# A fused audio tower on one core: the router's sigmoid by tanh, fewer small steps, and two states scaled by B on TensorE through diagonal matrices

## What is computed

```python
# 1. attention inside each segment, q = k = v
probs = softmax(einsum('bsqd,bskd->bsqk', x, x) / sqrt(256)); h = einsum('bsqk,bskd->bsqd', probs, x)
# 2. a selective scan on layernorm(h), 512 channels, 16 states n
x_in, z = split(xn @ W_in.T); x_conv = silu(conv4(x_in) + b_conv)
dt = softplus(x_conv @ W_dt.T + b_dt); B = x_conv @ W_B.T; C = x_conv @ W_C.T
state[n] = exp(dt * A[n]) * state[n] + dt * B[n] * x_conv;   y += C[n] * state[n]
h = h + (y * silu(z)) @ W_out.T
# 3. a mixture of 64 experts on layernorm(h)
scores = sigmoid(logits); sfc = scores + gate_bias     # 8 groups of 8 experts
# a group's score is the sum of its two best sfc; 4 groups are kept, then the 8 best experts of them
# weights: the kept scores over their sum, times 2.5; each expert runs silu(g) * u @ w_down
```

## Time and profile before

| | before |
|---|---|
| median of three runs | 3476.5 us (3473.83 to 3476.91) |
| the profiled execution | 3474.01 us, of which span 3472.2 us |
| PE busy | 2993.6 us, 86% |
| DVE busy | 2874.4 us, 83% |
| ACT busy | 2853.9 us, 82% |
| POOL busy | 2104.8 us, 61% |
| PE clock granted, mean | 0.955 |

### The profile page before, as it was taken

The page is one execution under the profiler, slowest core; times in us unless marked ns, Lnnn a source line. Parts: engine busy times, 40 slices in busy tenths (PEclk is TensorE's granted clock), DMA queues, the critical chain, the costliest instruction groups (busy, mean ns, idle before and its releaser), DMA issues. The chain is left out here.

```text
span 3472.2 us, 62460 instructions
## 1 busy us (share of the span) xinstructions
PE 2993.6 (86%) x19009; PEld 2407.9 (69%) x19009; DVE 2874.4 (83%) x4756; ACT 2853.9 (82%) x5580; POOL 2104.8 (61%) x780
## 2 busy tenths in 40 slices
PE   6899999999999999999999999999999997576664
PEld 4777777777777777777777777777777776455543
DVE  3888999999989999999999999999999998444432
ACT  5999999999999999999999999999999995211110
POOL 0666665666656565656565666666666665177776
PEclk8999999999999999999999999999999998578887
DMA  2111222111212121112221211111211110267774
GB/s 92 51 51 60 62 62 63 50 57 62 62 63 62 54 62 48 54 61 62 63 62 63 62 59 57 63 62 63 62 63 62 58 53 27 89 142 150 149 150 81
DMA packets 187542, 241.44 MB, mean 70 GB/s; under 512 B 45152, under 2 KB 165440, under 8 KB 187200
## 3 DMA queue, kind: packets, MB, share of 16 engines
q1 hardware_dynamic: 162624, 199.44, 18.5%
q0 software_dynamic: 24576, 37.77, 6.5%
HBM read 176.07 MB, written 61.08 MB: 68 GB/s over the span
## 5 line engine op out<-in xcount | busy, mean ns | idle before, releaser
L356 POOL TENSOR_TENSOR hid<-hid,c_all 128x1536 f32<-128x1536 f32 x512 | 1770.2, 3457 | 1160.9 <-DVEq L610 1159.4
L615 DVE TENSOR_TENSOR_SCAN hid<-decay,hid,psB 128x1024 f32<-128x1024 f32 x512 | 1201.6, 2347 | 101.8 <-PE psB L926 60.4
L386 ACT ACTIVATE decay<-dt,a_neg 128x383 f32<-128x383 f32 x2048 | 1086.7, 607 | 0.0
L374 ACT ACTIVATE dbu_t<-dtu_t,b_t 128x512 f32<-128x512 f32 x1536 | 994.6, 715 | 41.6 <-PE psB L926 38.1
L926 PE MATMUL psB<-ident,dbu_t 128*128 128x128 f32 x6144 | 856.9, 276 | 109.8 <-DVE hid L615 103.8
L926 PEld LDWEIGHTS psB<-ident,dbu_t 128*128 128x128 f32 x6144 | 701.5, 141 | 234.6 <-DVE hid L615 133.3
L938 PE MATMUL psY<-ident,hid 128*128 128x128 f32 x6144 | 765.3, 275 | 4.0 <-DVE yz_t L627 3.6
L938 PEld LDWEIGHTS psY<-ident,hid 128*128 128x128 f32 x6144 | 695.3, 142 | 6.9 <-issue 3.8
L615 DVE TENSOR_TENSOR_SCAN hid<-decay,psB 128x512 f32<-128x512 f32 x512 | 623.8, 1218 | 72.4 <-PE psB L926 29.7
L1013 PE MATMUL psM<-u,w_dt 128*128 128x384 f32 x1024 | 355.0, 490 | 21.2 <-ACT turned L396 16.8
L1013 PEld LDWEIGHTS psM<-u,w_dt 128*128 128x128 f32 x1024 | 184.4, 190 | 131.4 <-ACT turned L396 23.7
(11 more groups left out here) (149 smaller groups left out, 3348.3 us busy)
## 6 DMA issues: line engine op xcount, KB each, us to landing
c_all<-bc_rows_dram SPq DMA_DIRECT2D x128, 768.0 KB, 4.8
out_dram<-h SPq DMA_DIRECT2D x64, 384.0 KB, 5.6
h<-out_dram SPq DMA_DIRECT2D x32, 384.0 KB, 4.0
x_weights_dram<-normed SPq DMA_DIRECT2D x32, 384.0 KB, 3.3
xs<-in_x_dram SPq DMA_DIRECT2D x32, 256.0 KB
e_wg<-in_gate_dram SPq DMA_DIRECT2D x64, 128.0 KB
e_wu<-in_up_dram SPq DMA_DIRECT2D x64, 128.0 KB
e_wd<-in_down_dram SPq DMA_DIRECT2D x64, 128.0 KB
```

The source lines that it names most:

```text
L356: nc.gpsimd.tensor_tensor(hid[k % 4][:, :, :], hid[k % 4][:, :, :], c_all[:, k, :].unsqueeze(1).to_broadcast([P, CH, L]), ALU.mult).then_i ...
L374: last = nc.scalar.activation(dbu_t[k % 2][:, t, :], dtu_t[q][:, t, :], ACT.Copy, scale=b_t[q][:, t, k:k + 1])
L386: last = nc.scalar.activation(decay[k % 4][:, c, 1:L], dt[q][:, c, 1:L], ACT.Exp, scale=a_neg[:, c, k:k + 1])
L615: nc.vector.tensor_tensor_scan(h[:, lo:hi], flat(decay[k % 4])[:, lo:hi], flat(psB)[:, lo:hi], h[:, lo - 1:lo] if j else 0.0, ALU.mult, AL ...
```

## The change

1. **B by diagonal matrices.** For the states in `DIAG`, which are two of the 16 (4 and 10), ACT does no `scaled_dbu`. DVE writes `diag` (L734 of the changed kernel): for each such state and segment, the identity times B of the row, in a new step `spread_b`, once a sequence. PE forms the block of `psB` as a full matmul of `dtu_t` with the diagonal matrix instead of a transpose of `dbu_t`.
2. **Sigmoid.** ACT computes tanh(logit / 2) while the silu table is loaded, and DVE does one multiply-add; the add of one and the reciprocal go. For that, LG moves from slot 15 of sequence b - 2 to slot 4 of b - 3.
3. **Fewer small steps.** Newton's step for the norm takes three DVE instructions, not four. The row maximum is negated by the reduction itself, since 1/sqrt(D) now sits in the copies of QT0 and QT1. `score_groups` joins maxima that have the same operation.
4. **Softplus.** The four `Abs` on PSUM pieces become two on 128 x 768 in SBUF.
5. **Order.** O1 moves from slot 0 to slot 15 (its add to slot 0), the norm and routing on DVE one slot earlier, QT1 and its copy, `softplus(n, 0)`, `finish_dt(n, r, 0)` and the copies of xin, yz and dtu by up to one slot.

```diff
+DIAG = (4, 10,)
@@ scaled_dbu
                 after(act, s_bt, PB * (s - 1))
+                if k in DIAG:
+                    return
@@ DVE
+            def spread_b(n, r):
+                dve.wait_ge(s_out[slot("BT")], number("BT", n))
+                for i, k in enumerate(DIAG):
+                    last = nc.vector.tensor_tensor(diag[:, i, :, :], ident[:, :].unsqueeze(1).to_broadcast([P, NSEG, P]),
+                                                   b_t[r][:, :, k:k + 1].to_broadcast([P, NSEG, P]), ALU.mult)
+                last.then_inc(s_dg, 1)
@@ turn_dbu
-                    last = nc.tensor.transpose(flat(psB)[:, i * P:(i + 1) * P],
-                                               dbu_t[k % 2][:, t, c * P:(c + 1) * P], ident[:, :])
+                    if k in DIAG:
+                        last = nc.tensor.matmul(flat(psB)[:, i * P:(i + 1) * P], dtu_t[q][:, t, c * P:(c + 1) * P],
+                                                diag[:, DIAG.index(k), t, :], start=True, stop=True)
+                    else:
+                        last = nc.tensor.transpose(flat(psB)[:, i * P:(i + 1) * P],
+                                                   dbu_t[k % 2][:, t, c * P:(c + 1) * P], ident[:, :])
@@ ACT
-                nc.scalar.activation(soft[:, c, :], src, ACT.Abs, bias=b_dt[:, c:c + 1]).then_inc(s_out[slot(name)], 1)
+                nc.scalar.activation(soft[:, a:z, :], xin[:, a:z, TAPS - 1:], ACT.Abs).then_inc(s_de[half], 1)
-                    "p (s e) -> p s e", s=NSEG), ACT.Exp, scale=-1.0).then_inc(s_out[slot("LG")], 1)
+                    "p (s e) -> p s e", s=NSEG), ACT.Tanh, scale=0.5).then_inc(s_out[slot("LG")], 1)
@@ score_experts
-                nc.vector.tensor_scalar(flat(denom), flat(denom), 1.0, None, ALU.add).then_inc(s_rt, 1)
-                nc.vector.reciprocal(flat(score), flat(denom)).then_inc(s_rt, 1)
+                nc.vector.tensor_scalar(flat(score), flat(denom), 0.5, 0.5, ALU.mult, ALU.add).then_inc(s_rt, 1)
@@ newton
-                nc.vector.tensor_scalar(t[:, 2, :], t[:, 1, :], -0.5, 1.5, ALU.mult, ALU.add).then_inc(s_nw[j], 1)
@@ row_max
-                nc.vector.tensor_scalar(nmax[:, :], rmax[:, :], -(D ** -0.5), None, ALU.mult).then_inc(s_nm, 1)
```

More of the change, by code:

```diff
@@ L48, in after, with scaled_before @@
     eng.wait_ge(sem, count)
[L51 to L54, removed]
+DIAG = (4, 10,)
+SCALED = NS - len(DIAG)
+def scaled_before(k):
+    return k - sum(d < k for d in DIAG)
+SLOTTED = (("XN0", "X0", "X2", "Z0", "Z2", "D0", "D1", "D2", "D3", "X2T0", "AT0", "BT", "DU1", "DU2", "O1"),
+           ("XN1", "X1", "X3", "Z1", "LG", "QT0", "QT1", "S", "PT", "CB", "X2T1", "AT1", "YT0", "DU0", "YT1",
+            "YT2", "O0"))
 LAG = {**dict.fromkeys(("QT0", "QT1", "S", "PT", "AT0", "AT1",), 2),
@@ L109, in sequence_phase @@
         c_all = sb("c_all", [P, NS, L])
+        diag = sb("diag", [P, max(len(DIAG), 1), NSEG, P])
         decay = [sb(f"decay{j}", [P, CH, L]) for j in range(4)]
@@ L139, in sequence_phase @@
         rs0 = [sb(f"rs0{j}", [P, NSEG]) for j in range(2)]
-        nw = [sb(f"nw{j}", [P, 3, NSEG]) for j in range(2)]
+        nw = [sb(f"nw{j}", [P, 2, NSEG]) for j in range(2)]
         rstd = [sb(f"rstd{j}", [P, NSEG]) for j in range(2)]
@@ L395, in copy_turned @@
                 to = turned2 if name in ("X2T0", "X2T1") else turned
-                nc.scalar.activation(to[:, kd, :], psM[slot(name)][:, 0:L], ACT.Copy).then_inc(s_out[slot(name)], 1)
+                by = D ** -0.25 if name in ("QT0", "QT1") else 1.0
+                nc.scalar.activation(to[:, kd, :], psM[slot(name)][:, 0:L], ACT.Copy,
+                                     scale=by).then_inc(s_out[slot(name)], 1)
             def copy_xin(b, c):
@@ L421, in biased_dt @@
                 src = psM[slot(name)][:, 0:L]
-                nc.scalar.activation(xin[:, c, TAPS - 1:], src, ACT.Identity, bias=b_dt[:, c:c + 1])
-                nc.scalar.activation(soft[:, c, :], src, ACT.Abs, bias=b_dt[:, c:c + 1]).then_inc(s_out[slot(name)], 1)
+                nc.scalar.activation(xin[:, c, TAPS - 1:], src, ACT.Identity,
+                                     bias=b_dt[:, c:c + 1]).then_inc(s_out[slot(name)], 1)
             def softplus(n, half):
@@ L535, in body @@
                         if front:
+                            copy_xin(n, 1)
+                        if late:
+                            first_rstd(o, 1)
+                        if front:
                             copy_xin(n, 2)
@@ L550, in body @@
                             biased_dt(n, 1)
+                        if early:
+                            copy_turned("QT1", a, 1)
+                        if front:
+                            softplus(n, 0)
                     if k == 7:
@@ L553, in body @@
                             biased_dt(n, 2)
-                            softplus(n, 0)
-                        if late:
-                            copy_turned("X2T0", o, 0)
+                        if early:
+                            probs(a)
                     if k == 8:
@@ L751, in score_groups @@
-            def score_groups(m):
-                hi, lo = halves[:, 0, :, :], halves[:, 1, :, :]
-                hi2, mn, mx, lo2 = (quarters[:, j, :, :] for j in range(4))
+                routed_to(m, 2)
+                grp = biased[:, :, :].rearrange("p t (g h k) -> p (t g) h k", g=G, h=2)
+                nc.vector.tensor_tensor(halves[:, 0, :, :], grp[:, :, 0, :], grp[:, :, 1, :], ALU.max)
+                nc.vector.tensor_tensor(halves[:, 1, :, :], grp[:, :, 0, :], grp[:, :, 1, :], ALU.min).then_inc(s_rt, 1)
@@ L838, in body @@
                         nc.vector.engine_nop().then_inc(s_go, 1)
+                    if k == 0:
+                        if late:
+                            add_block(o, 1)
                     if k == 1:
                         if late:
[L841 removed]
                             second_stats(o)
@@ L1118, in body @@
                     if k == 8:
-                        if late:
-                            turn_normed2(o, 0)
                         if front:
@@ L1125, in body @@
                     if k == 9:
+                        if late:
+                            turn_normed2(o, 0)
                         if front:
```

192 lines of the change are left out of this document (93 added, 99 removed).

## The result

The changed kernel takes 3452.95 us in the median of four runs (3450.26 to 3454.04), the kernel before beside it 3476.7. The ratio is 0.9932, with a 95% interval of 0.9915 to 0.9949. That is 24 us faster. The profiled execution took 3450.26 us, of which the span is 3448.2. Against the profiled execution before (3474.01) it is 24 us too; forecast from there were 49.

A forecast was written before the change was run, and what follows sets the result against it. ACT was taken as the bound, DVE and PE close behind. Per sequence -0.3 and -1.3 make -1.6, over 31 sequences -50 us; with +1 at the end, 3474.0 becomes 3425 us, 8-in-10 range 3400 to 3481.

The forecast's parts named there:

- The step that failed: In the scan loop, ACT, idle 1.1 and 1.4 us in the two stretches, was taken as the bound.
- The dense stretch: Scan loop from PE's work at state 2 to state 10: 49.48 us to become 49.2, -0.3, with PE the bound.
- 48.9: PE's work in us between states 2 and 10 after the change: 45.7 before plus 3.2.
- 3.8 us of waits: PE's waits between states 2 and 10 before the change, the 49.48 us less 45.7 of work, expected to shrink to about 0.3.
- The light stretch: Scan loop from state 10 to the next state 2: DVE binds, 40.2 us to become 38.9, -1.3.
- 0.3 of waits: Allowance in us between state 10 and the next state 2, on top of DVE's 38.6, giving 38.9.
- The loop's turn stays: At the scan loop's turn no change in time was forecast; all gain was put in the 31 sequences.
- The end: After the last silu: two table loads on the last norm's chain +2.6, shorter last routing -1.6, sum +1 us.
- D: Rival: ACT still waits for the turning of state k - 2, halving the gain to 3450; counted with the forecast, together 0.71.
- A: Rival: PE's waits between states 2 and 10 stay, making the kernel slower, 3509 with 3.0 us left; chance 0.12.
- B: Rival: exchange without gain, PE waits of 1.5 to 2.2 us or DVE's ring remaining, within 7 us of 3474; chance 0.13.
- C: Rival: ACT alone bounds the scan loop, so the period falls by its full 3.8 us, to 3357; chance 0.04.

The follow-up runs named there:

- d_4: The changed kernel with only state 4 by a diagonal matrix instead of states 4 and 10: 3442.37 us, ratio 0.9907.
- d_10: The changed kernel with only state 10 by a diagonal matrix instead of states 4 and 10: 3471.33 us, ratio 0.9988.
- no state: The changed kernel without diagonal matrices and without spread_b, ACT scaling all 16 states again: 3456.5 us, ratio 0.9944.
- before_lg1: The kernel before with half of the router's product left out, 0.7 us less for PE, for timing alone: 3464.61 us, ratio 0.9976.
- before_norecip: The kernel before with the sigmoid's reciprocal replaced by a multiplication, 1.0 us less for DVE, for timing alone: 3463.92 us, ratio 0.9975.
- act_all: The changed kernel with ACT also scaling states 4 and 10, into a tile nobody reads, PE still using the diagonal matrices: 3485.13 us, ratio 1.0028.
- old_diag: The kernel before with only the diagonal matrices of states 4 and 10 added, in the old order: 3485.63 us, ratio 1.0036.
- After_lg1: The changed kernel with half of the router's product left out, 0.7 us less for PE, for timing alone: 3436.89 us, ratio 0.9897.
- d_3: The changed kernel with only state 3 by a diagonal matrix, instead of states 4 and 10: 3473.41 us, ratio 0.9997.
- Before_small: The kernel before with only the shorter Newton step and the negated row maximum, in the old order: 3472.63 us, ratio 0.9995.

## Why the prediction was off

**The costs.** Diagonal blocks 0.112 us apart, the multiplications on `diag` 0.543 us, `dbu_t` 14 times a sequence (1344 in all), two `Abs` at 0.85: all as forecast, and no table load at the tanh inside the loop. A state on `diag` keeps PE busy 195.8 / 64 = 3.06 us, against 752.8 / 448 = 1.68 for one of the other 14, a difference of 1.38 as forecast. The busy time of the engines moved less than the sums. ACT's fell by 3.1 us a sequence and not by 3.8: d_4 and d_10 have it 1.6 and 1.5 below no state, where 1.84 a state was put. PE's rose by 2.2 and not by 2.8, DVE's fell by 0.6 and not by 1.05. Where the rest went wasn't followed up.

**The step that failed** is the first: "ACT idles 1.1 and 1.4 us, less than either of the others, so ACT is the bound". From it came that both stretches shorten once ACT is relieved. In the kernel before, before_lg1 and before_norecip left ACT's work alone, and the ordinary period fell all the same by 0.26 and 0.32 us, which it could not if ACT's work alone set it. In the changed kernel, act_all measured the relief alone at 0.96 us for 3.1 removed, and the price on the other side at 1.13. (The relief alone was not measured in the kernel before; old_diag has relief and price together, +0.57.) The least idle engine was one of three that hand work round a ring: DVE scans a piece, PE may turn the next, ACT may write the one after. Removing work on one of them shows where another was waiting for it at that moment, and by the rows of no state these places are the X copies and the silu of Z. Ahead of them lies state 4's `dbu_t`, not state 10's.

**The dense stretch.** That PE becomes its bound was right, and PE busy over 98% too (49.58 of 49.90). The size of its work was not: "48.9" should be 49.6. The rows could have told: the earlier trace rows has PE busy 46.9 to 47.1 us in this stretch where the sum by the pace of each kind gave 45.7, and with the 3.2 forecast on top that is over 50 (2.6 came). What the prediction called 3.8 us of waits, to be won back, was 2.5 of idle time. So the stretch rose from 49.48 to 49.9 instead of falling by 0.3. After_lg1, with 0.7 us of PE's work less, has an ordinary period 0.52 shorter, which agrees with the bound. ACT idles 3.5 us there, less than the 4 forecast.

**The light stretch.** "That is -1.3" was wrong. My 40.2 for it before was too long, as its edges were not those of the 49.48: the ordinary period of 89.2 less the dense 49.48 leaves 39.7. After, 89.13 - 49.9 = 39.2. So -0.5 came, not -1.3. What was left as "0.3 of waits" is the wait for state 10's longer pieces alone, at 6.5 / 12 = 0.54 a sequence. The prediction's last sentence named this danger, DVE waiting at state 10; it had trusted DVE's work in those slots to hide it. For state 4 it does (no such wait is among the rows of d_4), for state 10 it does not.

**The loop's turn.** "The loop's turn stays" was wrong by 1.5 us a turn, some 19 in all, and this carries most of the gain. That the total came to half of the forecast is therefore luck: it is another gain than the one worked out. O1's new place explains the slot wait that is gone. It does not explain the turn: with O1 put back, the excess over an ordinary sequence is 1.16, not 2.35. State 10 has a part in it: the excess is 0.89 with it (changed kernel, d_10, act_all) and 1.22 to 1.31 without (no state, d_4, d_3), and old_diag has 1.67 in the old order. The rest, from 2.35 to 1.22, comes with the new order or the smaller parts, not with a shorter branch. Before_small, with two of the small steps, has 2.74 and so doesn't show it. Which part it is wasn't separated and stays open.

**The end.** Forecast were +1, measured are -3.9: from the last silu to the end of the scan 134.4 us pass in both kernels, and from there to the count phase 51.5 instead of 55.4. The phases behind it, which the change doesn't touch, were another 1.9 us shorter in the profile. Of the two table loads put on the chain, the one ahead of `lnv` is not on it. Timeline of ACT in the changed kernel:

```profile
2926.64 1.28 ACT L490 ACT_TABLE_LOAD   x1
2936.12 0.30 ACT L490 ACTIVATE lnv<-mv,epsc 128x3 f32<-128x3 f32 x1 [8.20 <-DVE mv L657]
2936.44 1.28 ACT L492 ACT_TABLE_LOAD   x1
2937.74 0.20 ACT L492 ACTIVATE rs<-lnv 128x3 f32<-128x3 f32 x1
```

The first load passes during a wait of 8.2 us for DVE. The second costs 1.30, from its start to that of the next. The Trainium skill, page "ScalarE: Activation LUTs", section "What ACT_TABLE_LOAD costs", counts 2.66 us with a drain; this row disagrees with that again. How the 3.9 us are made up wasn't tried.

**The rivals.** D hit the size (half, 3450) by luck, and not the cause: what ACT's relief gave was taken by the price on PE and DVE, and the gain that came is at the turns. A had the right sign for the dense stretch, which got longer, but with waits that did not stay. B, an exchange without gain, is what the ordinary sequences did. C is refuted by act_all: 3.1 us of ACT's work are worth 0.96.

## What to carry to other kernels

Where three engines hand work round a ring, the least idle of them is not yet the bound: look up, slot by slot, who waits for it, and relieve it only directly ahead of those waits. Before a trade between engines is spread over several places, try each place alone; here one state alone was worth -14 us and another +15. Read a loop's periods with a turn, right behind one, and away from one apart, and look which results share a PSUM slot before moving one.

## What was not expected of the hardware

- PE's branch at a turn of the loop takes 3.3 to 4.1 us in both kernels, those of DVE and ACT 0.06 and 0.05. What it costs depends on the work around it: 2.35 us over an ordinary sequence in the kernel before, 0.89 in the changed one. Seven turns fewer save 24 us (3.4 each) and 12.6 (1.8 each), more than this excess, as the sequence behind a turn is 0.3 to 0.4 us longer too.
- A full f32 matmul of 128 x 128 costs two records of 0.112 us, where a transpose of the same shape costs one of 0.109. Both ran with the granted clock at 1.00, in the light stretch too.
- With two sequences a turn, the ordinary periods of one kernel repeat to 0.05 us in all runs but one, while those with a turn vary from 90.7 to 92.7 us before and from 89.8 to 90.4 after.
